# A third PSUM bank for the exponentials' scores, two shared banks for projections and output path

## The chip, the cores and the metric

The kernel runs on one core of one Trainium2 chip. The metric is the device time of one execution in microseconds (us). A core has a matrix engine (TensorE, PE in the rows; PEld is its weight load), a vector engine (DVE), a scalar engine (ACT), GpSimd (POOL), a queue engine for transfers (SP), and an accumulation memory, PSUM, of eight banks of 128 partitions x 512 float32 values. Only PE's results go there; ACT and DVE read them out. PE may overwrite a bank only once the last reader of what stood there is done, and it waits for that on a semaphore. PE executes its instructions in the order written.

## The reference

Two cross-attention layers after each other, batch of 4, 256 queries and 512 keys of width 256. The first has 16 heads of width 16 and an MLP of width 1024; the second one head of width 256 and a residual scaled by alpha.

```python
x = layer_norm(hidden_states, ln1_w, ln1_b)
q, k, v = x @ q_w + q_b, ctx @ k_w + k_b, ctx @ v_w + v_b      # 16 heads of 16
attn = softmax(where(mask, q k^T * scale, min))
hidden = (attn @ v) @ cproj_w + cproj_b + residual
y = gelu(layer_norm(hidden, ln2_w, ln2_b) @ fc_w + fc_b, approximate=True) @ proj_w + proj_b
x = hidden + y
# second layer, w_q, w_k, w_v, w_o of 256 x 256
probs = softmax((x @ w_q.T) @ (ctx @ w_k.T).T / sqrt(256))
out = x + alpha * ((probs @ (ctx @ w_v.T)) @ w_o.T)
```

## The kernel before

The four batches run one after the other through a pipeline that is written out by hand. The attention of one batch takes 32 slots, 8 for each of 4 groups of 4 heads (`slots`, `attend`). In nearly every slot PE makes one score tile of 128x512 whose maximum is wanted (`max_tile`, L562, tile `s1`; in slots 0 and 1 of a group two of them, in slots 6 and 7 none) and one score tile for the exponentials (`exp_tile`, L579, two matmuls, tile `s2`). DVE reduces the first kind to row maxima (`take_max`, L1331), ACT exponentiates the second (`exp`, L1009). In slot 5 of a group DVE splits the maxima of the next group into three bf16 parts (`split_max`, L1341 to L1347), in slot 6 PE transposes them (`max_rows`, L569) and ACT copies them into the operand of the next group's exponentials (`rows`, L1000). Twice a group PE multiplies probabilities by values (`pv`, L589).

Into these slots are threaded, by tables that name the slot of each step:

- the projections of the next batch (`pre`, `PRE_AT`): the transposed context in two halves CT0 and CT1 (L538), the transposed normalised input ZT (L533), then Q, K0, K1, V0, V1 (helper line L504). CT0 is at slot 7, CT1 at 8, ZT at 9, Q at 11, K0 at 14, K1 at 22, V0 at 36, V1 at 38. ACT copies a transposed tile and DVE subtracts the copy from it (L1301); K0 and K1 are read by DVE alone (L1310); V0 and V1 by ACT (L982);
- the output path of the batch before (`post`, `POST_AT`): OT0 and OT1, the transposed attention output in two halves, at slot 7 (L625), divided by the softmax sums on DVE (L1366, L1368); NT, CP, ZT; the MLP's four chunks F0 to F3; its second product in four parts PJ0 (slot 20), PJ1, PJ2 (slot 23), PJ3 (slot 25), which add up in one bank; the second layer's transposed context in halves, here called post-CT0 at slot 22 and post-CT1 at slot 24 (L618); then HT, G, S0, S1, PT0, PT1, PC and DL. The matmuls of these steps stand at the helper lines L517 and L521. `LATE_AT` spreads the same steps out for the third batch.

PE's order within a slot is: maximum tiles, `pre`, `post`, the exponentials' tile, `pv`, `max_rows`. The other engines follow the same slots, but read out most `pre` and `post` tiles on DVE one slot later; in a slot DVE takes `pre` ahead of `post`. The slots from 7 of one batch to 6 of the next are one iteration. Iteration 0 has projections and the preparation of weights (`prepare`), but no output path. Iterations 1 and 2 have both. In iteration 3 there is no further batch to project: the last batch's own output path (`tail`) runs beside the third batch's.

PSUM before: `s1` has 2 banks, `s2` 2, `om` (the attention output and the transposed maxima) 1, `pre_ps` 1, `post_ps` 2. The table `POST_BANK` gives each step of the output path one of its two banks.

Of the kernel before, what the change touches and what calls it, by code (L numbers as in the profile page):

```python
# [103 lines left out]
POST_BANK = (0, 1, 0, 1, 0, 1, 0, 1, 0, 1, 0, 0, 0, 1, 0, 1, 0, 1, 0, 1)  # L104
# [22 lines left out]
def build(nc, x, ctx, mask, ln1_w, ln1_b, q_w, q_b, k_w, k_b, v_w, v_b, cproj_w, cproj_b, ln2_w, ln2_b,  # L127
          fc_w, fc_b, proj_w, proj_b, l1_q, l1_k, l1_v, l1_o, alpha, out):
    with ExitStack() as stack:
# [176 lines left out]
        def bank_of(n):  # L306
            return POST_BANK[n]

# [7 lines left out]

        def pre_bank(b, n):

            if b == 0:
                return (pre_ps[:], post_ps[:, 0, :], post_ps[:, 1, :])[pre_place(b, n) % 3]  # L320
            return pre_ps[:]

        def post_use(b, n):

            bank = bank_of(n)
            return bank, POST_BANK.count(bank) * b + POST_BANK[:n].count(bank) + 1

# [56 lines left out]

        def steps_at(b):
            return LATE_AT if b == B - 2 else POST_AT

        def pre_at(b):
            return EARLY_AT if isinstance(b, int) and b == 1 else PRE_AT
# [109 lines left out]
        def _(pe):  # L499
# [55 lines left out]
            def max_tile(b, g, s):  # L555
# [5 lines left out]
                await_(pe, s1_free, n - 1)  # L561
                pe.matmul(s1[:, s % 2, :], q_stack[0:ROW_MAX, hd, chunk(t)], k_stack[0:ROW_MAX, hd, :],  # L562
# [9 lines left out]
            def exp_tile(b, g, s):  # L572
# [3 lines left out]
                await_(pe, s2_free, n - 1)  # L576
                for i in range(2):
                    k = 2 * (s % 2) + i
                    mm = pe.matmul(s2[:, s % 2, i * LQ:(i + 1) * LQ], k_stack[:, hd, chunk(k)], q_stack[:, hd, :],  # L579
                                   start=True, stop=True)  # L580
# [13 lines left out]
            def post(b, step):  # L594
                def open_(n):

                    bank, count = post_use(b, n)
                    await_(pe, post_free[bank], count)
                    return post_ps[:, bank, :]
# [10 lines left out]
                def fill(mm, n):  # L610
                    mm.then_inc(post_full[bank_of(n)], 1)
# [44 lines left out]
                elif step[:2] == "PJ":  # L656
                    i = int(step[2])
                    pe.wait_ge(y_hi, 4 * b + i + 1)
                    o = open_(W_PJ) if i == 0 else post_ps[:, bank_of(W_PJ), :]
# [1166 lines left out]
```

## Time and profile before

| | |
|---|---|
| median of three runs | 322.81 us |
| lowest, highest of the three | 320.57, 324.02 us |
| the profiled execution's own time | 322.9 us |
| its profiled span | 321.1 us |
| PE busy | 272.4 us, 85% of the span |
| DVE busy | 219.6 us, 68% |
| ACT busy | 188.6 us, 59% |
| mean granted clock of TensorE | 0.946 of full speed |

The profiled execution lies 0.1 us from the median. Between span and time lie 1.8 us. A time row of the trace gives a start and a duration in us from the span's start; a bracket behind it gives how long the engine had been idle and who ended that.

### The profile page before, as it was taken

The page shows a single profiled execution, that of the slowest core. Times are in us where ns is not written, and L with a number is a line of the kernel's source. Part 1 is how long each engine was busy: PE and PEld are TensorE (multiplying, and loading weights), DVE is VectorE, ACT ScalarE, POOL GpSimd, SP SyncE. Part 2 cuts the span into 40 slices and gives each one's busy share as a digit, 9 for nine tenths or more (in the row PEclk, how much of TensorE's full clock was granted, in tenths as well). Part 3 has the DMA queues.
Part 4 walks back from the last instruction along what each step waited for, and adds up shares of the span by engine and source line. Part 5 has one row for each costly group of instructions (what it writes and reads, how often), then busy time and mean ns, then how long its engine had stood idle before and what let it go on. Part 6 is the DMA issues. An engine that isn't in the chain of part 4 may idle for free.

```text
span 321.1 us, 5439 instructions
## 1 busy us (share of the span) xinstructions
PE 272.4 (85%) x2065; PEld 195.5 (61%) x2065; DVE 219.6 (68%) x433; ACT 188.6 (59%) x351; POOL 87.7 (27%) x85
## 2 busy tenths in 40 slices
PE   2936759999797979998979899989899988868995
PEld 2722435583274758764956757647767766657884
DVE  6756865758679678866488598674868744645844
ACT  2541635748765695967365877673637785325522
POOL 3311001503001387530022576700012271123300
PEclk9995878996799999999999999999999999969999
DMA  6299990292172029002630182018110000000000
GB/s 192 98 126 174 132 357 15 51 130 77 49 100 100 0 56 167 37 0 69 82 133 0 28 120 39 0 38 113 62 72 2 0 2 2 1 0 0 2 33 33
DMA packets 21805, 21.59 MB, mean 67 GB/s; under 512 B 2962, under 2 KB 18916, under 8 KB 21780
## 3 DMA queue, kind: packets, MB, share of 16 engines
q1 hardware_dynamic: 19488, 17.25, 29.3%
q10 hardware_dynamic: 2292, 4.01, 3.6%
q8 instruction: 16, 0.26, 0.4%
q14 instruction: 9, 0.07, 0.1%
HBM read 10.50 MB, written 1.05 MB: 36 GB/s over the span
## 4 chain that ended last, share of the span: by engine, by line
PE 44%; DVE 21%; ACT 15%; SPq 7%; issue 5%; POOL 4%; DMA 3%; ACTq 1%; DVEq 0%
PE post_ps L517 8%; PE om L589 7%; PE pre_ps L504 6%; DVE neg_max L1331 5%; PE s L562 4%; PE s L579 4%; PE post_ps L521 4%; ACT q_stack L1000 3%; ACT probs L1009 3%; SPq L431 2%; SPq L441 2%; PE s L517 2%; DMA cx<-in_ctx_dram 2%; DVE ft L1414 1%; DVE cT_l L1301 1%
## 5 line engine op out<-in xcount | busy, mean ns | idle before, releaser
L1331 DVE TENSOR_REDUCE neg_max<-s 128x1 f32<-128x512 f32 x128 | 83.2, 683 | 19.6 <-PE s L562 18.8
L1009 ACT ACTIVATE probs<-s 128x512 f32<-128x512 f32 x128 | 75.8, 599 | 23.9 <-PE s L579 23.4
L562 PE MATMUL s<-k_stack,q_stack 97*128 97x512 bf16 x128 | 49.7, 418 | 13.9 <-DMA q_stack<-qp 7.3
L579 PE MATMUL s<-q_stack,k_stack 109*128 109x256 bf16 x256 | 51.2, 283 | 2.7 <-ACT q_stack L1000 2.2
L562 PEld LDWEIGHTS s<-k_stack,q_stack 97*128 97x128 bf16 x128 | 12.6, 99 | 38.7 <-DVE neg_max L1331 20.2
L589 PE MATMUL om<-probs,vals 128*17 128x256 f32 x512 | 36.0, 404 | 0.0
L579 PEld LDWEIGHTS s<-q_stack,k_stack 109*128 109x128 bf16 x256 | 21.1, 101 | 16.3 <-ACT q_stack L1000 4.3
L1663 POOL TENSOR_TENSOR ln<-ln,minus_half 128x2 f32<-128x2 f32 x8 | 5.6, 704 | 82.8 <-DVE ln L1279 82.8
L1000 ACT ACTIVATE q_stack<-om 13x1024 bf16<-13x1024 bf16 x16 | 16.3, 1017 | 9.7 <-PE om L569 9.3
L589 PEld LDWEIGHTS om<-probs,vals 128*17 128x17 f32 x512 | 12.2, 100 | 14.5 <-issue 7.8
L1357 DVE TENSOR_TENSOR y_l<-post_ps,y_h 128x512 fp32r<-128x512 f32 x12 | 8.3, 689 | 16.2 <-ACT y_h L1023 16.2
L1023 ACT ACTIVATE y_h<-post_ps 128x512 fp32r<-128x512 f32 x12 | 7.0, 596 | 17.0 <-PE post_ps L521 13.7
L1414 DVE SCALAR_TENSOR_TENSOR ft<-ft,fx 128x512 f32<-128x512 f32 x9 | 12.0, 1333 | 7.2 <-POOL ft L1718 7.2
L1723 POOL TENSOR_TENSOR y_l<-fx,y_h 128x512 fp32r<-128x512 f32 x9 | 11.6, 1283 | 14.8 <-ACT y_h L1062 14.8
L1683 POOL TENSOR_TENSOR kf<-kf,kp 128x512 f32<-128x512 f32 x7 | 8.1, 1161 | 23.5 <-ACT kp L992 23.5
L1718 POOL TENSOR_TENSOR ft<-fx 128x512 f32<-128x512 f32 x9 | 9.4, 1043 | 15.6 <-ACT fx L1036 15.6
L517 PE MATMUL post_ps<-aT_h,wf_h 128*128 128x256 f32 x48 | 13.6, 316 | 0.0
L517 PE MATMUL post_ps<-wp_h,y_h 128*128 128x256 f32 x48 | 13.5, 313 | 0.1
L1705 POOL TENSOR_TENSOR h<-h,cb 128x512 f32<-128x512 f32 x3 | 3.8, 1277 | 32.7 <-DMA h<-in_x_dram 32.7
L517 PE MATMUL post_ps<-wp_l,y_h 128*128 128x256 f32 x48 | 11.8, 280 | 0.0
L517 PE MATMUL post_ps<-aT_h,wf_l 128*128 128x256 f32 x48 | 11.8, 280 | 0.0
L1687 POOL TENSOR_TENSOR kp<-kf,kp 128x512 bf16<-128x512 f32 x7 | 9.2, 1321 | 3.8 <-ACT kp L996 3.8
(327 smaller groups left out, 704.5 us busy)
## 6 DMA issues: line engine op xcount, KB each, us to landing
k_stack<-kp SPq DMA_DIRECT2D x48, 128.0 KB
q_stack<-qp SPq DMA_DIRECT2D x48, 64.0 KB
cx<-in_ctx_dram SPq DMA_DIRECT2D x4, 512.0 KB, 5.8
pcx<-in_ctx_dram ACTq DMA_DIRECT2D x3, 512.0 KB, 3.6
xz<-in_x_dram SPq DMA_DIRECT2D x5, 256.0 KB, 5.5
raw_late<-in_L_xattn_fc_w_dram SPq DMA_DIRECT2D x1, 1024.0 KB, 8.0
raw_late<-in_L_xattn_proj_w_dram SPq DMA_DIRECT2D x1, 1024.0 KB, 10.1
h<-in_x_dram ACTq DMA_DIRECT2D x3, 256.0 KB, 2.7
```

The source lines that it names most:

```text
L504: mm = pe.matmul(o, wi(w[a], k), vi(v[c], k), start=start and k == 0 and i == 0, stop=stop and k == n - 1 and i == 2)
L517: pe.matmul(o, wi(w[a], k), vi(v[c], k), start=start and i == k == a == c == 0, stop=False)
L521: mm = pe.matmul(o, wi(w[late[0]], k), vi(v[late[1]], k), start=False, stop=stop and i == len(terms) - 1 and k == n - 1)
L562: pe.matmul(s1[:, s % 2, :], q_stack[0:ROW_MAX, hd, chunk(t)], k_stack[0:ROW_MAX, hd, :], start=True, stop=True).then_inc(s1_full, 1)
L579: mm = pe.matmul(s2[:, s % 2, i * LQ:(i + 1) * LQ], k_stack[:, hd, chunk(k)], q_stack[:, hd, :], start=True, stop=True)
L589: mm = pe.matmul(om[32 * j:32 * j + VW, 0:LQ], vals[:, k, g * GH + j, :], probs[:, g % 2, j, k, :], start=k == 0, stop=k == TK - 1)
L1000: act.activation(q_stack[ROW_MASK:ROWS, g * GH:(g + 1) * GH, :], om_rows[ROW_MASK:ROWS, :].unsqueeze(1).to_broadcast([ROWS - ROW_MASK, GH, ...
L1009: act.activation(probs[:, g % 2, s // 2, k:k + 2, :], s2[:, s % 2, :].rearrange("p (k n) -> p k n", k=2), ACT.Exp).then_inc(s2_free, 1)
L1331: dve.tensor_reduce(neg_max[:, g % 2, s % 2, s // 2:s // 2 + 1], s1[:, s % 2, :], AX.X, ALU.max, negate=True).then_inc(s1_free, 1)
L1414: dve.scalar_tensor_tensor(f, f, 1.0 / GELU_CUBIC, fx[i % 3], ALU.add, ALU.mult).then_inc(cube, 1)
L1718: pool.tensor_tensor(ft[i % 3], fx[i % 3], fx[i % 3], ALU.mult).then_inc(square, 1)
L1723: pool.tensor_tensor(lo, fx[i % 3], hi.bitcast(F32), ALU.subtract).then_inc(y_split, 1)
```

## The change

All eight banks were in use and still are. `s2` gets a third bank. `pre_ps` and `post_ps` go, and a tile `work_ps` of two banks takes their place. A function `work_uses` lists every use of these two banks in PE's order (projections of the next batch, output path, three steps of the weight preparation) and deals them out in turn; while PJ0 to PJ3 add up in one bank, every other use goes to the other. `await_bank` makes each use wait until the use before it on its bank has been read out. The exponentials' tiles go round three banks in batches 0 to 2 and round two in batch 3, where the third serves the last output path. The first batch's projections use the third `s2` bank for every third tile and `work_ps` for the rest.

```diff
-POST_BANK = (0, 1, 0, 1, 0, 1, 0, 1, 0, 1, 0, 0, 0, 1, 0, 1, 0, 1, 0, 1)
...
-        s2 = ps("s2", [P, 2, 512])
+        s2 = ps("s2", [P, 3, 512])
         om = ps("om", [P, 512])
-        pre_ps = ps("pre_ps", [P, 512])
-        post_ps = ps("post_ps", [P, 2, 512])
-        tail_banks = [pre_ps[:], s1[:, 0, :], s1[:, 1, :], s2[:, 0, :], s2[:, 1, :], om[:]]
+        work_ps = ps("work_ps", [P, 2, 512])
+        spare_ps = s2[:, 2, :]
+        tail_banks = [spare_ps, s1[:, 0, :], s1[:, 1, :], s2[:, 0, :], s2[:, 1, :], om[:]]
...
+                    for use in new:
+                        bank = 1 - held if held is not None else 1 - bank
+                        uses.append(use + (bank,))
+                        if use[0] == "post" and use[2] == W_PJ:
+                            held = bank
+                    if step == "PJ3":
+                        held = None
...
+        def await_bank(eng, kind, b, n):
+
+            bank = work_bank(kind, b, n)
+            on = [u for u in WORK if u[3] == bank]
+            at = [u[:3] for u in on].index((kind, b, n))
+            if at == 0:
+                return
+            kind, b, n, _ = on[at - 1]
+            if kind == "pre":
+                eng.wait_ge(pre_free, PRE_USES if b == 0 else pre_use(b, n))
+            elif kind == "post":
+                eng.wait_ge(post_free[bank], post_use(b, n)[1] + 1)
...
+        def s2_bank(b, s):
+
+            return s % 2 if b == B - 1 else (NS * b + s) % 3
...
             def pre(b, n):
 
                 at = pre_place(b, n)
+                if b > 0:
+                    await_bank(pe, "pre", b, n)
                 await_(pe, pre_free, PRE_USES * b + n if b > 0 else max(at - 2, DC if n == U_K else U_ZT + 1) if n > U_ZT else at - 2)
...
-                await_(pe, s2_free, n - 1)
+                await_(pe, s2_free, s2_before(b, SLOTS * g + s))
...
-                    bank, count = post_use(b, n)
-                    await_(pe, post_free[bank], count)
-                    return post_ps[:, bank, :]
+                    await_bank(pe, "post", b, n)
+                    return work_ps[:, work_bank("post", b, n), :]
```

No instruction changes its place on any engine, and none is added but waits. Dealt out in turn, the uses of iteration 1 (and of 2, with the same banks) are, as bank 1: CT0, OT1, NT, CP, ZT of the output path, K0, F2, PJ, HT, S0, PT0, V0, DL; as bank 0: OT0, CT1, ZT of the projections, Q, F0, F1, F3, K1, post-CT0, post-CT1, G, S1, PT1, PC, V1. A projection keeps its old wait for the projection before it and gets the bank's wait beside it.

PE's rows at slots 7 and 8 of iteration 1, before (L538 is CT0, then CT1; L625 is OT0, then OT1; the semaphores in brackets are what the row waits for):

```order
L538 MATMUL pre_ps<-ident,cx 128x128 x3
L625 MATMUL post_ps<-ident,oT 128x128 [waits post_free0,o_done]
L625 MATMUL post_ps<-ident,oT 128x128 x3
L625 MATMUL post_ps<-ident,oT 128x128 [waits post_free1]
L625 MATMUL post_ps<-ident,oT 128x128 x3
L579 MATMUL s<-q_stack,k_stack 128x256 [waits s2_free]
L579 MATMUL s<-q_stack,k_stack 128x256
L562 MATMUL s<-k_stack,q_stack 128x512 [waits s1_free,stacked1]
L562 MATMUL s<-k_stack,q_stack 128x512 [waits s1_free]
L538 MATMUL pre_ps<-ident,cx 128x128 [waits cx_in,pre_free]
```

The same place in the change (L607 for L538, L696 for L625):

```order
L607 MATMUL work_ps<-ident,cx 128x128 x3
L696 MATMUL work_ps<-ident,oT 128x128 [waits pre_free,o_done]
L696 MATMUL work_ps<-ident,oT 128x128 x3
L696 MATMUL work_ps<-ident,oT 128x128 [waits pre_free]
L696 MATMUL work_ps<-ident,oT 128x128 x3
L651 MATMUL s<-q_stack,k_stack 128x256 [waits s2_free]
L651 MATMUL s<-q_stack,k_stack 128x256
L631 MATMUL s<-k_stack,q_stack 128x512 [waits s1_free,stacked1]
L631 MATMUL s<-k_stack,q_stack 128x512 [waits s1_free]
L607 MATMUL work_ps<-ident,cx 128x128 [waits cx_in,pre_free,post_free0]
```

OT1 waited for the output path's own bank and now waits for the projections' CT0 to be read out; CT1 waits for OT0 as well.

PE's rows at slots 22 and 23 of iteration 1, before (L504 is the end of K1, L618 post-CT0, L569 the transposed maxima, L517 the start of PJ2):

```order
L504 MATMUL pre_ps<-cT_h,wk_l 128x512
L618 MATMUL post_ps<-ident,pcx 128x128 [waits post_free0,pcx_in]
L618 MATMUL post_ps<-ident,pcx 128x128 x3
L579 MATMUL s<-q_stack,k_stack 128x256 [waits s2_free]
L579 MATMUL s<-q_stack,k_stack 128x256
L569 MATMUL om<-ident_b,max_cols 109x128 [waits o_done,max_split]
L569 MATMUL om<-ident_b,max_cols 109x128
L517 MATMUL post_ps<-wp_h,y_h 128x256 [waits y_hi]
```

The same place in the change:

```order
L571 MATMUL work_ps<-cT_h,wk_l 128x512
L689 MATMUL work_ps<-ident,pcx 128x128 [waits pre_free,pcx_in]
L689 MATMUL work_ps<-ident,pcx 128x128 x3
L651 MATMUL s<-q_stack,k_stack 128x256 [waits s2_free]
L651 MATMUL s<-q_stack,k_stack 128x256
L638 MATMUL om<-ident_b,max_cols 109x128 [waits o_done,max_split]
L638 MATMUL om<-ident_b,max_cols 109x128
L584 MATMUL work_ps<-wp_h,y_h 128x256 [waits y_hi]
```

Nothing moved; post-CT0 waited for the output path's bank 0 and now waits for K1, the use right ahead of it, to be read out by DVE, since PJ holds the other bank.

## Rows read from the trace of the kernel before

**Rows 1.** The page: the span, and each engine's busy us.

```profile
span 321.1 us, 5439 instructions
PE 272.4 (85%) x2065; PEld 195.5 (61%) x2065; DVE 219.6 (68%) x433; ACT 188.6 (59%) x351; POOL 87.7 (27%) x85
```

**Rows 2.** Windows, iterations 1 and 2: busy us of PE, PEld, DVE, ACT, POOL; clock; DMA.

```profile
94.00:161.00 67.00, 60.77 (x499) 44.52 (x497) 49.01 (x97) 44.35 (x84) 24.14 (x20) 1.00 0.33 62
161.00:228.00 67.00, 60.73 (x498) 44.47 (x497) 49.38 (x98) 44.37 (x84) 25.42 (x21) 1.00 0.31 57
```

**Rows 3.** Waits of PE: waiting line, released by; us in total, times, longest.

```profile
PE s L579 <- ACT probs L1009: 0.4, 2, 0.2
```

**Rows 4.** Line L579, PE and PEld together: idle us before it, times, until.

```profile
  ACT probs L1009: 2.6, 8
```

**Rows 5.** Timeline of PE, iteration 0: start, us, what, idle before and releaser.

```profile
54.80 0.38 PE L579 MATMUL s<-q_stack,k_stack 109*128 109x256 bf16 x2
...
55.02 0.38 PE L562 MATMUL s<-k_stack,q_stack 97*128 97x512 bf16 x1
...
55.56 0.11 PEld L579 LDWEIGHTS s<-q_stack,k_stack 109*128 109x128 bf16 x2 [0.55 <-ACT probs L1009]
```

**Rows 6.** Timeline, iteration 1, slots 7 and 8.

```profile
95.51 1.04 PE L625 MATMUL post_ps<-ident,oT 128*128 128x128 f32 x8
...
97.15 0.69 DVE L1301 TENSOR_TENSOR cT_l<-pre_ps,cT_h 128x512 fp32r<-128x512 f32 x1 [0.50 <-ACT cT_h L966]
...
97.89 0.66 PE L538 MATMUL pre_ps<-ident,cx 128*128 128x128 f32 x4 [0.69 <-DVE cT_l L1301]
...
98.38 0.25 DVE L1366 RECIPROCAL rden<-post_ps 128x16 f32<-128x16 f32 x1
98.59 0.60 ACT L966 ACTIVATE cT_h<-pre_ps 128x512 fp32r<-128x512 f32 x1 [0.98 <-PE pre_ps L538]
...
99.00 1.28 DVE L1331 TENSOR_REDUCE neg_max<-s 128x1 f32<-128x512 f32 x2
```

**Rows 7.** Timeline, iteration 1, slots 22 and 23.

```profile
128.75 0.40 PE L504 MATMUL pre_ps<-cT_h,wk_l 128*128 128x512 f32 x1
...
128.99 0.60 PE L618 MATMUL post_ps<-ident,pcx 128*128 128x128 f32 x4
...
129.42 0.39 PE L579 MATMUL s<-q_stack,k_stack 109*128 109x256 bf16 x2
...
130.14 0.32 PE L569 MATMUL om<-ident_b,max_cols 128*109 128x128 bf16 x2 [0.34 <-DVE max_cols L1347]
...
130.60 0.74 DVE L1310 SCALAR_TENSOR_TENSOR kf<-pre_ps,bk,mask_f 128x512 f32<-128x512 f32 x1
```

**Rows 8.** Chain that ended last, iteration 1: start, us, what.

```profile
130.14 0.32 PE om L569 x2
130.46 1.00 PE post_ps L517 x8
```

**Rows 9.** Timeline, iteration 2, slot 23.

```profile
197.55 0.74 DVE L1310 SCALAR_TENSOR_TENSOR kf<-pre_ps,bk,mask_f 128x512 f32<-128x512 f32 x1
```

**Rows 10.** Timeline, iteration 1: K0's reader on DVE, start of F2.

```profile
113.43 0.74 DVE L1310 SCALAR_TENSOR_TENSOR kf<-pre_ps,bk,mask_f 128x512 f32<-128x512 f32 x1
...
114.54 0.47 PE L517 MATMUL post_ps<-aT_h,wf_h 128*128 128x256 f32 x1
```

**Rows 11.** Windows, as rows 2; the third number from the end is the granted clock.

```profile
70.00:94.00 24.00, 21.63 (x149) 10.58 (x149) 17.47 (x32) 17.32 (x28) 2.56 (x2) 0.79 0.45 85
...
264.00:267.00 3.00, 1.30 (x19) 0.81 (x11) 2.71 (x4) 1.34 (x4) 1.08 (x1) 1.00 0.00 0
...
283.00:290.00 7.00, 6.05 (x28) 5.71 (x29) 1.35 (x4) 1.44 (x3) 1.04 (x1) 0.51 0.00 0
```

**Rows 12.** Timeline of PE: two long idle times in iteration 3.

```profile
266.22 0.41 PE L756 MATMUL s<-ident,mask_f 128*128 128x128 f32 x2 [1.70 <-DVE mask_f L1578]
...
283.17 1.09 PE L777 MATMUL s<-ident,mask_f 128*128 128x128 f32 x4 [2.32 <-DVE mask_f L1285]
```

More of the change, by code:

```diff
@@ L315, in pre_use, with work_uses @@
             return PRE_USES * b + pre_place(b, n) + 1
+        def work_uses():
+            uses, bank, held = [], 1, None
+            for n in FIRST_ORDER:
+                if pre_place(0, n) % 3:
+                    uses.append(("pre", 0, n, pre_place(0, n) % 3 - 1))
+            for b in range(B):
+                for at in range(START, LAST_SLOT if b == B - 1 else START + NS):
+                    new = []
+                    if b < B - 1 and at in pre_at(b + 1):
+                        new.append(("pre", b + 1, pre_at(b + 1)[at]))
+                    if b < B - 1 and at in V_AT:
+                        new.append(("pre", b + 1, U_V + V_AT[at]))
+                    step = steps_at(b - 1).get(at) if b > 0 else None
+                    new += [("post", b - 1, n) for n in STEP_USES.get(step, ())]
+                    if b == 0 and PREP_AT.get(at) in PREP_USES:
+                        new.append(("prep", 0, PREP_AT[at]))
+                    for use in new:
[5 more added lines that the diff above has]
+                        held = None
+            return uses
@@ L317, in pre_bank, with work_bank @@
+        WORK = work_uses()
+        def work_bank(kind, b, n):
+            return [u[3] for u in WORK if u[:3] == (kind, b, n)][0]
         def pre_bank(b, n):
-            if b == 0:
-                return (pre_ps[:], post_ps[:, 0, :], post_ps[:, 1, :])[pre_place(b, n) % 3]
-            return pre_ps[:]
+            if b == 0 and pre_place(b, n) % 3 == 0:
+                return spare_ps
+            return work_ps[:, work_bank("pre", b, n), :]
         def post_use(b, n):
-            bank = bank_of(n)
@@ L326, in post_use @@
-            return bank, POST_BANK.count(bank) * b + POST_BANK[:n].count(bank) + 1
+            bank = work_bank("post", b, n)
+            return bank, [u[1:3] for u in WORK if u[0] == "post" and u[3] == bank].index((b, n)) + 1
+        def await_bank(eng, kind, b, n):
[9 more added lines that the diff above has]
+                eng.wait_ge(post_free[bank], post_use(b, n)[1] + 1)
+            elif n == "WO":
+                eng.wait_ge(w_lo, 4)
+            else:
+                eng.wait_ge(prep_done, 1 if n == "WT" else 2)
@@ new lines, in s1_bank, with s1_before, s2_before @@
+        def s1_bank(b, s):
+            return s % 2
+        def s1_before(b, s):
+            n = NS * b + s
+            return max([i for i in range(max(0, n - 3), n) if s1_bank(i // NS, i % NS) == s1_bank(b, s)], default=-1) + 1
+        def s2_bank(b, s):
+            return s % 2 if b == B - 1 else (NS * b + s) % 3
+        def s2_before(b, s):
+            n = NS * b + s
+            return max([i for i in range(max(0, n - 3), n) if s2_bank(i // NS, i % NS) == s2_bank(b, s)], default=-1) + 1
@@ L1052, in exp1 @@
                 act.wait_ge(cx_split, b + 1)
-                act.activation(probs1(b)[:, t, :], post_ps[:, bank, :], ACT.Exp, bias=stat1[:, 0, t:t + 1],
+                act.activation(probs1(b)[:, t, :], work_ps[:, bank, :], ACT.Exp, bias=stat1[:, 0, t:t + 1],
                                accum_out=stat1[:, 1, t:t + 1]).then_inc(post_free[bank], 1)
```

72 lines of the change are left out of this document (39 added, 33 removed).

## The prediction

> **What bounds the kernel now.** The page's busy times come first [rows 1]: PE works 272.4 of 321.1 us, DVE 219.6, ACT 188.6. PE is the busiest, and its share is an average. The windows by stage show that iterations 1 and 2 take 67 us each, with PE busy for 60.77 and 60.73 us at full granted clock [rows 2]. So in the two iterations where the output path and the next projections share the change's two banks, PE has only some 6 us to spare, and a wait put on PE there will mostly be added to the time. The second view is PE's waits, read for the one wait that a third score bank takes away: an exponentials' tile that waits for ACT to read an older one. PE's matmuls sat idle for it twice, 0.4 us in all [rows 3]; with the weight loads, which carry the semaphore and often wait while PE still streams the matmul ahead, it is 2.6 us in 8 places [rows 4]. The third view is the timeline at every use of the shared banks. For each I compared the start of the use with the end of the instruction that reads out the use now ahead of it on its bank. Where the start is later, the new wait is covered. It is clearly earlier at two places in an iteration, OT1 at slot 7 [rows 6] and post-CT0 at slot 22 [rows 7]. The chain of work that ended last passes through the second [rows 8].
>
> **The third score bank: 0.3 us gained.** What it can give is bounded by nothing from below (if PE's pause only moves to the next wait) and by the 2.6 us of rows 4 from above. I looked for places where the chain goes from an exponential to the next exponentials' tile. There is one: in iteration 0 the tile of slot 13 starts at 55.56 with its weight load idle for 0.55 us [rows 5]. The matmul ahead of it starts at 55.02, and a step from a pair of exponentials' matmuls to the next instruction is 55.02 - 54.80 = 0.22 us, so with a free bank it starts at 55.24, 0.3 us earlier. In iterations 1 and 2 PE reaches its exponentials' tiles later than ACT frees the banks. There the third bank gives nothing at first hand. I take 0.3 us.
>
> A rule of the Trainium skill speaks for more: Perfetto Trace Analysis, section Optimization Strategy, says that the same gap repeating on the engine that should be saturated can mean there is not enough PSUM for the next tile. Were the 2.6 us of rows 4 such gaps, the change would give 2.6 us by that rule; by the rows on PE's matmuls it is 0.4 us, so these are not the gaps that matter here.
>
> **OT1 waits for the projections' CT0: 0.2 us lost, twice.** The eight transposes of OT0 and OT1 run together from 95.51 to 96.55. CT0 is read out when DVE's subtraction ends, 97.15 + 0.69 = 97.84, and PE starts what waited for that 0.05 us later, at 97.89 [rows 6]. OT1 therefore starts at 97.89 instead of about 95.95. Queued behind it on PE are the exponentials' tile, the two maximum tiles of slot 8, and CT1, which itself waits until 97.89 today. PE's new order from 97.89: OT1 takes 0.43 (as post-CT0's four transposes from 128.99 to 129.42 [rows 7]), the exponentials' tile 0.22, the two maximum tiles 0.22 each, so CT1 starts at 98.98, 1.1 us later than now. But the chain runs over DVE here. Its reciprocal for OT1 starts at 98.38 [rows 6]; OT1 is now full at 97.89 + 0.60 = 98.49, so with a few hundredths for the signal it starts at about 98.57: 0.2 us later. Behind it the two reductions of 1.28 us now start at 99.20 and end at 100.48. ACT copies CT1 at 98.59 + 1.1 = 99.69 to 100.29, before DVE is free to use it. So CT1's 1.1 us are hidden by the two reductions, with 0.2 us to spare; without that cover it would be 1.1 us. I take 0.2, with 1.1 as upper end and 0 as lower (if DVE catches up in a later pause).
>
> **Post-CT0 waits for K1: 1.9 us lost, twice.** K1's last matmul ends at 128.75 + 0.40 = 129.15, and PE goes on with post-CT0 at 128.99. K1 is read out by DVE one slot later, after the row maxima of the next group have been split and after a step of the MLP's gelu: from 130.60 to 131.34 [rows 7]. PJ holds the other bank, so post-CT0 may start at 131.34 + 0.05 = 131.39, 2.4 us later. Queued behind it on PE are the exponentials' tile of slot 22 and the transposes of the maxima, which start at 130.14, as soon as DVE has split them. Now they start at 131.39 + 0.43 + 0.22 = 132.04: 1.9 us later. What DVE does until 131.34 needs nothing that stands behind the wait, so the 131.34 stays. The transposes are on the chain, and what follows on the chain is PE itself, part PJ2 [rows 8]; on ACT the copy of post-CT0, the exponential and the copy of the maxima queue up and come 2.5 us late, but ACT is idle for a third of this iteration (44.35 of 67 [rows 2]) and need not carry that on. The stall of 1.9 us thus runs through to the end. Iteration 2 shows the same pattern 66.95 us later: DVE's reading of K1 starts at 197.55 [rows 9] against 130.60. So twice 1.9 = 3.8 us. The lower end is 1.0 each (third rival), the upper 2.4, the whole delay of post-CT0.
>
> **The other uses: nothing.** The other new neighbours on a bank are covered in the trace. The tightest is F2, which starts at 114.54 where K0 is read out at 113.43 + 0.74 = 114.17 [rows 10]: 0.4 us of cover. All of them move together with the delays above, so the cover stays; if F2's were gone it would be some tenths, since ACT is the later one there. In iteration 3 there are no projections to share with, and iteration 0 has no output path. 17 waits are added in front of PE's groups, 10 of them in iterations 1 and 2. A group with two waits starts no later in these rows than one with one, so they cost nothing at best; at worst the 0.2 us of a step each, 2 us.
>
> **Sum.** 322.9 (the profiled execution's own time) - 0.3 + 2 x 0.2 + 2 x 1.9 = 326.8 us. The median of the three runs is 322.8, so the same sum from there gives 326.7. I predict 326.8. This case's own range is 325.2 to 328.6: less 1.6 for stalls that are partly absorbed, more 1.8 for OT1's missing cover (2 x 0.9).
>
> **Rivals.**
>
> *The clock falls.* The new pause of PE ahead of post-CT0 is 131.39 - 129.15 = 2.2 us long. In iteration 3 an idle time of 1.70 us left the granted clock at 1.00, and one of 2.32 us [rows 12] stands ahead of a stretch of 7 us at 0.51 [rows 11], which is the lower level, 1.2 GHz. The new pause lies between, nearer the longer. Against it: ahead of the 2.32 us PE had been idle in several more places, while ahead of post-CT0 it works without a gap. A stretch of 7 us at half the clock where PE is busy nine tenths of the time costs 7 x 0.49 = 3.4 us: 330.2 us if it happens once, 333.6 if in both iterations. Chance 16 in 100. The page TensorE: Matmul & The Clock Gate of the Trainium skill, section A second HAM failure mode: psum-queue depth-cycling, says that a kernel whose PE paused briefly between groups while it cycled through PSUM banks went back and forth between the two clock levels; here the trace of before, with pauses such as 0.69 and 0.34 us [rows 6, 7], shows the granted clock at 1.00 in both iterations [rows 2].
>
> *The stall is partly absorbed.* Iterations 1 and 2 have some 6 us each in which PE is idle [rows 2]. If later pauses of PE belong to chains that the delay doesn't touch, they swallow part of it, and about 1 us of each 1.9 is left: 322.9 - 0.3 + 0.4 + 2.0 = 325.0 us, within 1%. Against it speaks that the chain is on PE itself right behind the stall. Chance 20 in 100.
>
> *Faster: PE runs ahead in iteration 0.* The stretch from 70 to 94 us has a mean granted clock of 0.79 [rows 11]; the missing 0.21 of 24 us are 5.0 us. If the third bank closes the pauses of the weight loads (2.6 us) and with them keeps the clock up, the kernel gains 7.6 us against 4.2 lost: 319.5 us. It decides from a gain of 7.4 us on (3.2 for the 1% and 4.2 for the stalls), so nearly all of both would have to come. The chain crosses this stretch with ACT's exponentials and weight copies back to back, and a bank makes ACT no faster. Chance 6 in 100.
>
> **How the numbers follow.** My forecast has 56 in 100, the rivals 16, 20 and 6, and 2 are left for what I don't see. A measurement of this kernel tells about 1% from no change: below 319.6 is faster, above 326.0 slower. Of the 56, about 44 lie above 326.0 and 12 below; with the clock's 16 and 1 of the rest, slower is 0.61, within 1% is 0.12 + 0.20 + 0.01 = 0.33, faster 0.06. The range for 8 in 10 goes from 323.9 (the absorbed case, with a further microsecond) to 330.4 (the clock falling once).
>
> **What the changed kernel's profile would show.** If I am right: PE's row for the transposes of post-CT0 has an idle time of about 2 us released by DVE's read of K1, once in each of iterations 1 and 2; OT1's four transposes stand apart from OT0's with about 1.7 us of idle time, and CT1's no longer wait; the reductions behind OT1 are 0.2 us late; iterations 1 and 2 are each about 2 us longer than 67 and iteration 0 is as long as before within 0.5 us; PE no longer waits for ACT ahead of exponentials' tiles. The prediction is wrong if the granted clock falls in iterations 1 or 2, if iteration 0 becomes shorter by more than 1 us, or if the delay at slot 22 is there and the iteration has its old length.

## The result, and the profile after

The changed kernel took 330.72 us (median of 4 executions, 328.67 to 334.46) beside 321.88 us for the kernel before: a ratio of 1.0223, with a 95% interval of 1.0169 to 1.0277. (The ratio leaves out executions in a slower state, here the profiled one; the two medians alone would give 1.027.)

Measured again later, with more executions, it was 333.12 us, ratio 1.034 [1.0287, 1.0392]. The two intervals of the same kernel don't touch, so a difference of about 0.01 between two kernels that were not measured together says nothing. A part of it can be the clock: the mean granted clock of the three executions in the first ratio is 0.940, that of the six in the second 0.927. Ratios are compared below. e1, e2, e3 and e5 were measured together on one chip, e4, e6, e7 and e8 on a second, e9 to e12 on a third.

The profiled execution took 334.46 us, 3.7 above its median, so a sum made on its trace must be read against that; the trace of the second measurement (335.12 us, the same granted clock of 0.917) looks alike.

The page after, as [rows 1]. PE's busy time rises by 7 us with the same 2065 matmuls; DVE, ACT and POOL do what they did.

```profile
span 332.7 us, 5456 instructions
PE 279.5 (84%) x2065; PEld 203.2 (61%) x2065; DVE 220.4 (66%) x433; ACT 188.3 (57%) x351; POOL 87.6 (26%) x85
PEclk9975858969797999999989998999999997968999
```

The same PEclk line of the page of the kernel before (40 slices, granted clock in tenths):

```profile
PEclk9995878996799999999999999999999999969999
```

The mean granted clock of the profiled execution is 0.917, where the kernel before had 0.946. The windows of iterations 1 and 2, to be held against [rows 2], and of three short stretches, against [rows 11] (columns: stretch, its length, busy us of PE, PEld, DVE, ACT, POOL, granted clock, DMA share, GB/s):

```profile
96.00:166.50 70.50, 61.96 (x497) 45.60 (x495) 49.27 (x96) 44.33 (x84) 24.15 (x20) 0.98 0.29 58
166.50:237.00 70.50, 62.06 (x487) 45.57 (x486) 48.41 (x93) 43.84 (x83) 25.46 (x21) 0.95 0.29 53
...
99.80:103.20 3.40, 3.40 (x16) 2.74 (x16) 2.35 (x5) 1.05 (x2) 0.00 (x0) 0.51 0.33 82
171.50:174.90 3.40, 3.32 (x15) 2.26 (x14) 2.46 (x5) 1.88 (x4) 0.44 (x1) 0.50 0.59 158
205.70:209.10 3.40, 3.40 (x19) 3.28 (x17) 0.69 (x1) 2.73 (x4) 0.09 (x1) 0.51 0.02 5
```

These windows are cut by hand. By the ends of the same exponentials' tiles in both traces, iterations 1 and 2 are 3.8 and 4.9 us longer than before, not 2. The three short stretches stand at 1.2 GHz, the lower level, right behind three of the four new pauses. PE is busy through all of them (3.32 to 3.40 of 3.40 us), and the trace of the second measurement has the same three, at 100.3, 171.9 and 206.1. The waits of PE (line, releaser: us in total, times, longest):

```profile
PE work_ps L689 <- DVE kf L1383: 4.7, 2, 2.3
PE work_ps L696 <- DVE cT_l L1374: 3.5, 2, 1.8
```

These are post-CT0, which waits for K1's reader, and OT1, which waits for CT0's reader. The row of [rows 3], exponentials' tiles that wait for ACT, has no answer after: that wait is gone. Timeline of iteration 1, slots 7 and 8, as [rows 6] (start, us, engine, line, what; in brackets the idle time before it and the releaser):

```profile
97.25 0.60 PE L696 MATMUL work_ps<-ident,oT 128*128 128x128 f32 x4
...
98.87 0.69 DVE L1374 TENSOR_TENSOR cT_l<-work_ps,cT_h 128x512 fp32r<-128x512 f32 x1 [0.56 <-ACT cT_h L1039]
99.62 0.95 PE L696 MATMUL work_ps<-ident,oT 128*128 128x128 f32 x4 [1.76 <-DVE cT_l L1374]
100.37 0.63 PE L651 MATMUL s<-q_stack,k_stack 109*128 109x256 bf16 x2
100.61 0.26 DVE L1439 RECIPROCAL rden<-work_ps 128x16 f32<-128x16 f32 x1 [0.43 <-PE work_ps L696]
101.47 1.29 DVE L1404 TENSOR_REDUCE neg_max<-s 128x1 f32<-128x512 f32 x2
101.65 1.06 PE L607 MATMUL work_ps<-ident,cx 128*128 128x128 f32 x4
```

OT0's four transposes took 0.60 us, and OT1's, the same work behind 1.76 us of idle time, 0.95. The exponentials' tile behind them took 0.63, where 0.39 stands in [rows 7], and CT1's four transposes 1.06 instead of 0.66 [rows 6]. These rows lie in the stretch at 0.51. Slots 22 and 23 of iteration 1, as [rows 7]:

```profile
134.10 0.75 DVE L1383 SCALAR_TENSOR_TENSOR kf<-work_ps,bk,mask_f 128x512 f32<-128x512 f32 x1
134.99 0.63 PE L689 MATMUL work_ps<-ident,pcx 128*128 128x128 f32 x4 [2.33 <-DVE kf L1383]
135.68 0.28 PE L638 MATMUL om<-ident_b,max_cols 128*109 128x128 bf16 x2
```

The chain that ended last, as [rows 8] (start, us, what), now enters the place over DVE's reading of K1:

```profile
134.18 0.67 DVE kf L1383
134.85 0.14 issue
134.99 0.63 PE work_ps L689 x4
135.62 0.22 PE s L651 x2
135.84 0.11 PE om L638 x2
135.95 1.00 PE work_ps L584 x8
```

Comparing the end of every exponentials' tile between the two traces shows where the 11.6 us (332.7 - 321.1) of the profiled execution arise: iteration 0 1.7 (the tiles fall behind where a low-clock stretch starts at 69.1 instead of 71.4), OT1 1.8 in iteration 1 and 1.4 in iteration 2, post-CT0 2.0 in iteration 1 and 3.6 in iteration 2, the last iteration about 1.2 (a low-clock stretch from 277.3 that the kernel before doesn't have).

### The profile page after: what moved, and what is told of

Same layout as the page of the kernel before. It is cut to its first block, busy times and chain, and to the rows that moved or that the text cites. A ratio compares the mean times of both kernels' runs of the same rounds, so it can differ in the third digit from the quotient of the medians.

```text
span 332.7 us, 5456 instructions
## 1 busy us (share of the span) xinstructions
PE 279.5 (84%) x2065; PEld 203.2 (61%) x2065; DVE 220.4 (66%) x433; ACT 188.3 (57%) x351; POOL 87.6 (26%) x85
## 4 chain that ended last, share of the span: by engine, by line
PE 47%; DVE 20%; ACT 14%; SPq 6%; issue 5%; POOL 4%; DMA 3%; ACTq 1%; DVEq 0%
PE work_ps L584 9%; PE om L661 7%; DVE neg_max L1404 5%; PE s L631 5%; PE s L651 4%; PE work_ps L588 4%; PE work_ps L571 4%; ACT probs L1082 3%; SPq L498 2%; SPq L508 2%; PE s L584 2%; ACT q_stack L1073 2%; DMA cx<-in_ctx_dram 2%; DVE ft L1487 1%; PE work_ps L925 1%
## 5 line engine op out<-in xcount | busy, mean ns | idle before, releaser
L651 PE MATMUL s<-q_stack,k_stack 109*128 109x256 bf16 x256 | 52.2, 290 | 2.2 <-ACT q_stack L1073 2.1
L661 PE MATMUL om<-probs,vals 128*17 128x256 f32 x512 | 35.2, 396 | 0.0
L651 PEld LDWEIGHTS s<-q_stack,k_stack 109*128 109x128 bf16 x256 | 22.1, 104 | 15.5 <-ACT q_stack L1073 4.2
L1430 DVE TENSOR_TENSOR y_l<-work_ps,y_h 128x512 fp32r<-128x512 f32 x12 | 8.3, 689 | 16.2 <-ACT y_h L1096 16.2
L1796 POOL TENSOR_TENSOR y_l<-fx,y_h 128x512 fp32r<-128x512 f32 x9 | 11.6, 1285 | 20.0 <-ACT y_h L1135 20.0
L1096 ACT ACTIVATE y_h<-work_ps 128x512 fp32r<-128x512 f32 x12 | 7.0, 596 | 17.0 <-PE work_ps L588 13.7
L584 PE MATMUL work_ps<-wp_h,y_h 128*128 128x256 f32 x48 | 14.7, 335 | 0.0
L584 PE MATMUL work_ps<-aT_h,wf_h 128*128 128x256 f32 x48 | 13.6, 316 | 0.0
L584 PE MATMUL work_ps<-wp_l,y_h 128*128 128x256 f32 x48 | 13.1, 300 | 0.0
L584 PE MATMUL work_ps<-aT_h,wf_l 128*128 128x256 f32 x48 | 11.8, 280 | 0.0
L1430 DVE TENSOR_TENSOR pT_l<-work_ps,pT_h 128x512 fp32r<-128x512 f32 x6 | 4.2, 692 | 11.1 <-ACT pT_h L1100 11.0
```

The costliest lines, as they stand in the source:

```text
L584: pe.matmul(o, wi(w[a], k), vi(v[c], k), start=start and i == k == a == c == 0, stop=False)
L651: mm = pe.matmul(s2[:, s2_bank(b, SLOTS * g + s), i * LQ:(i + 1) * LQ], k_stack[:, hd, chunk(k)], q_stack[:, hd, :], start=True, stop=True)
L661: mm = pe.matmul(om[32 * j:32 * j + VW, 0:LQ], vals[:, k, g * GH + j, :], probs[:, g % 2, j, k, :], start=k == 0, stop=k == TK - 1)
L1430: dve.tensor_tensor(dst, work_ps[:, work_bank("post", b, n), :].rearrange("p (c n) -> p c n", c=dst.shape[1]), hi.bitcast(F32), ALU.subtra ...
L1796: pool.tensor_tensor(lo, fx[i % 3], hi.bitcast(F32), ALU.subtract).then_inc(y_split, 1)
```

## The experiments

Two theories stood against each other at the start. **A, waits alone:** the added time is the sum of the two pauses, and the banks' order sets it. **B, waits and clock:** a pause is paid once as a wait, and often again as a stretch at half clock behind it. (In the recorded expectations "Theory A" is the name of the view stated there, mostly that the two waits, with or without their clock, carry the loss. A and B below are the two of this paragraph.) A third question ran beside them: does the third score bank give anything? In e1 to e5 and e11 the exponentials' tiles use two banks again, and the eighth bank, called spare, is free for other use.

### Only the third score bank undone

`e1_two_score_banks`: the change with two score banks, the eighth bank idle. `e6_change_again` is the second measurement of the change itself, on another chip than e1.

```diff
-            return s % 2 if b == B - 1 else (NS * b + s) % 3
+            return s % 2
```

> The change with the third score bank left unused by the exponentials (two banks as in the kernel before), the two shared banks kept: what is left is the sharing alone. Theory A (the loss is two waits on the shared banks, OT1 and post-CT0, and the low-clock stretches that they bring; the third bank gives nothing): slower than before by the same 7 us as the change, within 1 us. Rival (the third bank gives the 2.6 us of weight-load waits and hides part of the sharing's cost): about 2.5 us slower than the change, 9.5 us over before.

> The change itself once more, beside the other three on one chip. By its first measurement 7.2 us over before (ratio 1.022). The kernel with two score banks gave a ratio of 1.033. Theory A (the third score bank gives nothing): here it comes out at 1.033 as well, within 0.005. Rival (the third bank gives about 3 us, more than the 0.3 us of the prediction): 1.022 again.

Measured: 332.35 us, ratio 1.0326 [1.0276, 1.0375], against 1.034 [1.0287, 1.0392] of the change. **The third bank gives nothing that can be measured**; the first measurement of the change, 1.0223, lies lower than both, so a gain is only possible as far as that difference between the two measurements leaves it open. The loss, 10.5 us here where 7 were expected, is there without the third bank, so it belongs to the two shared banks. The wait of PE for K1's reader in e1, and the windows behind its two pauses (columns as above):

```profile
PE work_ps L689 <- DVE kf L1383: 4.7, 2, 2.3
```

```profile
132.00:135.40 3.40, 2.67 (x23) 2.54 (x24) 1.27 (x2) 1.99 (x3) 0.00 (x0) 1.00 0.00 0
...
203.00:206.40 3.40, 3.40 (x19) 3.24 (x17) 0.69 (x1) 2.74 (x4) 0.37 (x1) 0.50 0.02 5
```

The same pause ahead of post-CT0 (2.34 us in each iteration) is followed by full clock in iteration 1 and by 3.4 us at half clock in iteration 2. The delay that arises there, by the ends of the exponentials' tiles, is 1.98 us in the first case and 3.55 in the second. One trace thus holds both prices: 2.0 for the wait, 1.6 more where a fall follows. The 1.6 is one pair of cases; e2, with a fall in both iterations, has 3.55 and 3.51. OT1's wait adds 0.27 us at once in both iterations.

### Each disputed use in a bank of its own

On top of e1, the spare bank takes the projections' CT0 (e2), K1 (e3) or both (e4) of batches 2 and 3, and nothing waits for or behind them.

```diff
+        def spared(kind, b, n):
+            return kind == "pre" and b >= 2 and n in (U_CT,)         # e3: (U_K + 1,)   e4: (U_CT, U_K + 1)
...
+                    new = [u for u in new if not spared(*u)]
...
-            if b == 0 and pre_place(b, n) % 3 == 0:
+            if spared("pre", b, n) or b == 0 and pre_place(b, n) % 3 == 0:
...
-                if b > 0:
+                if b > 0 and not spared("pre", b, n):
```

> As the run with two score banks, but the projections' CT0 of batches 2 and 3 goes to the idle eighth bank, so that OT1 no longer waits for it to be read out. Theory A with the prediction's price (OT1's wait costs 0.2 us an iteration beside the clock): 0.4 us faster than with two score banks, if the clock stays as it is. Theory A with the clock (the 1.8 us pause ahead of OT1 is followed by a stretch at the lower clock in both iterations, 3.5 us at half speed): 3 us faster, PEclk 1.00 after 94 us up to the second wait. Rival (sharing costs are spread over all uses): no change over 0.5 us.

Measured: 331.32 us, 1.0269 [1.0217, 1.032]; 0.006 less than e1, 1.8 us, with intervals that overlap, so that it does not decide between the expected 0.4 and 3 us. Here the clock fell in iteration 1 too, and post-CT0's wait cost 3.55 us there instead of e1's 1.98. Window of e2:

```profile
131.50:134.90 3.40, 3.29 (x16) 3.20 (x17) 0.69 (x1) 2.11 (x4) 0.00 (x0) 0.50 0.02 5
```

> As the run with two score banks, but K1 of batches 2 and 3 goes to the idle eighth bank, so that post-CT0 no longer waits for DVE to read it. Theory A: the 2.3 us pause ahead of post-CT0 goes in both iterations, 2 x 1.9 = 3.8 us faster than with two score banks, up to 1.6 us more where a low-clock stretch followed. Rival (the delay is absorbed later): under 2 us faster.

Measured: 324.63 us, 1.0067 [1.0029, 1.0106]. **Taking K1 alone out of the shared banks gives back 1.0326 - 1.0067 = 0.026, 8.4 us.** That is more than the 3.8 to 5.4 us expected. Its windows of iterations 1 and 2 stand at full clock, and by the tiles' ends they are 0.4 and 0.8 us longer than before:

```profile
94.00:162.00 68.00, 61.36 (x504) 45.15 (x503) 49.76 (x100) 44.42 (x86) 24.18 (x20) 1.00 0.33 62
162.00:229.00 67.00, 59.86 (x492) 43.78 (x491) 48.88 (x96) 44.30 (x84) 25.42 (x21) 1.00 0.31 56
```

> Two score banks, and both CT0 and K1 of batches 2 and 3 in the eighth bank, so that neither OT1 nor post-CT0 waits. All other uses still share two banks. Theory A (two waits carry all of the loss): the time of before, within 1 us. Rival (the other shared uses and the added waits of PE cost too): 2 us or more over before. The run that freed K1 alone was 2.2 us over before; if OT1's wait is the rest, this one is 1.5 to 2 us faster than that.

Measured: 323.9 us, 1.004 [1.001, 1.0071]. All the other shared uses and added waits together are worth 1.3 us, 0.3 to 2.3 by the interval. 8.4 us is twice what two waits of 2 us can explain. But it does not yet say that the rest is the clock, because an own bank also removes whatever else hangs on the wait.

### The waits kept, the pauses filled

`e5_fill_pauses`: e1 with every wait in its place, and ahead of each of the four waiting groups matmuls that nobody reads, into the spare bank. Their results are not used, so nothing that is computed changes. The first loop stands ahead of post-CT0, the second ahead of OT1.

```diff
+                    if c == 0 and b < B - 2:
+                        for _ in range(18):
+                            pe.matmul(spare_ps[:, 0:LQ], wq[0][:, 0, 0:P], wq[0][:, 0, :], start=True, stop=True)
...
+                        if t == 1 and b < B - 2:
+                            for _ in range(14):
+                                pe.matmul(spare_ps[:, 0:LQ], wq[0][:, 0, 0:P], wq[0][:, 0, :], start=True, stop=True)
```

> As the run with two score banks, with matmuls that nobody reads into the idle eighth bank right ahead of the two waits (14 of 128x256 ahead of OT1, 18 ahead of post-CT0, about 1.65 and 2.1 us at the higher clock), so that PE waits equally long but busy. This separates the wait from the clock. Theory A with the clock: no low-clock stretch behind 94 us before the last iteration, and 2 to 3 us faster than with two score banks, about 4.2 us over before, as the prediction's sum had it. Theory A without the clock (the low stretches come anyway, wherever they fall): the same time as with two score banks, or up to 1 us slower.

Measured: 326.0 us, 1.0128 [1.0086, 1.017]. Timeline of iteration 1:

```profile
128.37 2.32 PE L689 MATMUL s<-wq_h 128*128 128x256 f32 x18
130.79 0.66 PE L692 MATMUL work_ps<-ident,pcx 128*128 128x128 f32 x4
131.50 0.28 PE L638 MATMUL om<-ident_b,max_cols 128*109 128x128 bf16 x2
```

and the windows of iterations 1 and 2:

```profile
92.00:162.00 70.00, 65.30 (x537) 49.31 (x536) 49.84 (x101) 44.96 (x87) 24.17 (x20) 1.00 0.36 65
162.00:232.00 70.00, 65.27 (x538) 49.24 (x537) 50.19 (x99) 44.42 (x85) 25.42 (x21) 1.00 0.29 54
```

Post-CT0 is as late as in e1 (the delays are 1.94 and 1.93 us), and the clock stays at 1.00. **With the waits unchanged and the pauses filled, 1.0326 becomes 1.0128, 6.4 us less.** This tells A from B: the waits alone don't make the 10.5 us (0.0326 x 322.7) of e1. What the filled kernel costs, 0.0128 x 322.7 = 4.1 us, is about what the sum of the prediction had for the waits.

The split into 6.4 us of clock and 4.1 us of waits is that of whole executions, and not all of the 6.4 arises behind the four pauses. The mean granted clock is 0.927 over the six executions of e1, 0.953 over those of e5, and 0.946 over the 17 of the kernel before on that chip. With 2 x (1 - clock) x span, an estimate of the time at half clock, these are 48, 30 and 35 us. Four stretches of 3.4 us are 13.6 of the 18 us between e1 and e5, so part lies elsewhere, and e5 even has less of it than the kernel before. In the two traces iterations 1 and 2 together are 6.7 us longer than before in e1, with one fall, and 4.6 in e5; a further 1.9 us lie in iteration 0, where both run the same program. So it is shown that the lower clock costs e1 several us beside its waits; how much of that belongs to the four pauses stays open.

`e11_k1_own_fill_ot1` is e3 with the 14 matmuls ahead of OT1.

> Two score banks, K1 in the eighth bank, and 14 matmuls that nobody reads ahead of OT1's wait, so that OT1's pause stays and its idle time goes. With K1's own bank alone the ratio was 1.0067, with both in own banks 1.004. If OT1's wait costs through the clock: 1.004 here too, or less. If it costs through its delay alone: 1.007.

Measured: 323.75 us, 1.0028 [0.9994, 1.0062], beside e3's 1.0067 [1.0029, 1.0106]: about 1.3 us less, as B has it, but the intervals overlap and the chips differ, so this shows nothing by itself.

### Moving the output path instead

`e7_move_ct0` leaves the banks as in the change and puts post-CT0 two slots later, behind K1's reader; `e8_move_both` also puts the projections' CT0 a slot later, behind OT.

```diff
-           21: "PJ1", 22: "CT0", 23: "PJ2", 24: "CT1", 25: "PJ3", 26: "CX", 27: "HT", 28: "G", 30: "S0",
+           21: "PJ1", 23: "PJ2", 24: "CT0", 25: "PJ3", 26: "CT1", 27: "HT", 28: "G", 29: "CX", 30: "S0",
...
-PRE_AT = {7: U_CT, 8: U_CT + 1, 9: U_ZT, 11: U_Q, 14: U_K, 22: U_K + 1}
+PRE_AT = {8: U_CT, 9: U_CT + 1, 10: U_ZT, 12: U_Q, 14: U_K, 22: U_K + 1}
```

(The second pair of lines is e8's alone. Its expectation says that batches 1 and 3 follow this table; in fact batch 1 has the early table, and batches 2 and 3 follow this one, in iterations 1 and 2.)

> The change with three score banks, and the steps of the second layer's context moved in the table: post-CT0 from slot 22 to 24, post-CT1 from 24 to 26, CX from 26 to 29. DVE has read K1 by slot 23, so post-CT0 finds its bank free without a bank of its own. Theory A: the same gain as from K1's own bank, 5 to 8 us faster than the change, the idle time ahead of post-CT0 gone. Rival (the delay moves on: CX at 29 makes the second layer's exponentials at slot 31 wait for POOL's subtraction of 2.4 us): under 3 us faster, with a wait at the transposes PT0.

Measured: 333.57 us, 1.031 [1.0247, 1.0373], where 5 to 8 us less than the change were expected. A miss. The pause ahead of post-CT0 was gone, and a new one stood ahead of the transposes of the maxima. Timeline of e7, iteration 1:

```profile
140.80 2.34 POOL L1806 TENSOR_TENSOR pc_l<-pcx,pc_h 128x1024 fp32r<-128x1024 f32 x1 [6.96 <-ACT pc_h L1147]
140.86 2.31 DVE L1416 TENSOR_TENSOR max_rest<-neg_max,max_cols 128x8 f32<-128x8 f32 x1
143.65 0.32 PE L638 MATMUL om<-ident_b,max_cols 128*109 128x128 bf16 x2 [2.42 <-DVE max_cols L1420]
```

DVE's subtraction of 8 elements, 0.17 to 0.18 us elsewhere, took 2.31: it ended with POOL's large subtraction, and the transposes of the maxima waited 2.42 us for it. In iteration 2 they waited 3.43 us: there the same subtraction took 2.31 us again, and the cast behind it (L1418, also 128x8) took 1.20 instead of 0.18, beside a POOL instruction of 1.26 us on `xz`. The move gave one pause of PE for another.

> As the run with moved post-CT0, and the projections' CT0, CT1, ZT and Q of batches 1 and 3 one slot later (8, 9, 10, 12), so that OT0 and OT1 take the two banks first and CT0 follows when OT0 has been read. Batch 2 keeps its early slots by its own table, so OT1's wait goes in one of the two iterations. Theory A: 0.3 to 1 us faster than with post-CT0 moved alone. Rival: the shift puts Q's reading and F0 onto each other and costs 1 us or more.

Measured: 336.95 us, 1.0453 [1.0408, 1.0497]. The worst of all: it keeps e7's pauses, and in place of OT1's comes one of 1.62 us ahead of the transposes of z in each iteration, and in iteration 1 one of 2.02 ahead of a maxima tile.

`e9_swap` exchanges post-CT0 with the next PJ parts; `e12_before_swap` makes the same exchange in the kernel before.

```diff
-           21: "PJ1", 22: "CT0", 23: "PJ2", 24: "CT1", 25: "PJ3", 26: "CX", 27: "HT", 28: "G", 30: "S0",
+           21: "PJ1", 22: "PJ2", 23: "CT0", 24: "CX", 25: "PJ3", 26: "CT1", 27: "HT", 28: "G", 30: "S0",
```

> The change, with PJ2 in slot 22 and post-CT0 in slot 23 instead of the other way round; CX goes from 26 to 24 and post-CT1 from 24 to 26, so that the order of the other steps stays. PJ2's 1.5 us of matmuls then stand where PE waited for K1 to be read. Theory A: the pause of 2.3 us ahead of post-CT0 goes and nothing takes its place; what is left is OT1's wait: ratio to before 1.005 to 1.012, as with K1's own bank (1.007). Rival (DVE's row maxima or the transposes come later behind PJ2 and the loss stays): over 1.02.

> The kernel before with the same exchange of PJ2 and post-CT0 (and CX, post-CT1 at 24 and 26). PE then has PJ2 to do while DVE splits the maxima (idle 0.34 us at 129.81 in the trace of before). Expected: the same time within 1 us; at best 2 x 0.3 us faster, at worst 2 x 0.9 us slower, since the transposes of the maxima come behind PJ2's 1.5 us.

Measured: e9 333.81 us, 1.0348 [1.0296, 1.0399]; e12 333.2 us, 1.0315 [1.0263, 1.0366]. Both expectations were missed. The order of e9 costs the kernel before, which has three banks for these uses, 10 us of its own. With that order, going to two banks costs 0.0033 more, within the intervals. So what two banks cost hangs on which use stands next to which, and most of this order's loss is not that of the change. It comes from another pause. Waits, timeline and chain of e12:

```profile
PE s L562 <- DVE neg_max L1331: 10.9, 18, 2.2
```

```profile
132.50 1.21 PE L562 MATMUL s<-k_stack,q_stack 97*128 97x512 bf16 x2 [2.20 <-DVE neg_max L1331]
```

```profile
130.52 0.61 ACT pT_h L1027
131.15 0.69 DVE pT_l L1357
131.84 0.60 DVE neg_max L1331
132.50 1.21 PE s L562 x2
```

DVE now reads post-CT0 before it reduces the maxima, and PE waits 2.2 us for the maxima's bank. The two matmuls behind that pause take 1.21 us, twice the 0.60 of full clock (0.38 and a step of 0.22, [rows 5]): the low clock again, in the kernel with the old banks. By the tiles' ends each of e12's iterations 1 and 2 is 4.8 us longer than before. Some 1.3 us of that arise at slot 27 and not in e9: `POST_BANK` gives post-CT1 and HT the same bank, the exchange brings post-CT1 to the slot right ahead of HT's, and HT's transposes wait 1.07 us for DVE to read post-CT1 (139.57). So e9 and e12 lose by pauses that are in part different ones, and 0.0033 is not the pure price of two banks in this order.

`e10_swap_three_s1` is e9 with the third bank given to the maxima's tiles; the exponentials have two, and the waits on the spare bank follow it.

```diff
-        s1 = ps("s1", [P, 2, 512])
-        s2 = ps("s2", [P, 3, 512])
+        s1 = ps("s1", [P, 3, 512])
+        s2 = ps("s2", [P, 2, 512])
...
         def s1_bank(b, s):
 
-            return s % 2
+            return s % 2 if b == B - 1 or b == 0 and s < SLOTS else (NS * b + s) % 3
```

> As the run with PJ2 and post-CT0 exchanged, but the third score bank serves the maximum tiles that DVE reduces, and the exponentials have two. The trace of before has PE idle for 6.4 us ahead of maximum tiles and 0.4 us ahead of exponentials' tiles. If a bank is worth what PE waits for: up to 6 us faster than the exchange alone, 3 us faster than before. If the chain is DVE's own work there, so that PE's running ahead changes nothing (what the exponentials' bank showed for ACT): the same as the exchange alone within 1 us.

Measured: 330.75 us, 1.0257 [1.0199, 1.0315], some 3 us (0.0091 x 322.9) under e9, with intervals that just overlap. PE's waits for the maxima in e9, and then in e10:

```profile
PE s L631 <- DVE neg_max L1404: 10.8, 19, 2.1
```

```profile
PE s L633 <- DVE neg_max L1406: 7.6, 13, 1.5
PE work_ps L691 <- DVE kf L1385: 2.1, 2, 1.0
```

The last row shows that PE in e10 reaches post-CT0 early enough to wait for K1's reader again, 1.0 us each time. None of the experiments' kernels is faster than the kernel before; e11 is level with it.

### How often the clock fell

Pauses of 1.76 or 1.77 us ahead of OT1 (14 in seven traces: the change twice, e1, e3, e7, e9, e10) were followed 7 times by a stretch of 3.4 us at 0.50 or 0.51. Pauses of 2.33 to 2.36 us ahead of post-CT0 (8 in the change twice, e1 and e2) were followed by one 5 times: once in 4 in iteration 1, 4 in 4 in iteration 2. The 12 other pauses above 1.5 us in iterations 1 and 2 (e7 to e10 and e12) were followed by one 6 times: not those of 2.42 and 3.43 us in e7, but those of 2.1 to 2.2 us in e9 and e12, the 3.44 us of e8's iteration 2, and the one of 1.53 us in e10. A stretch is counted where it begins up to 1.5 us behind the pause's end, or in e12 up to 0.3 us ahead of it. Behind the places that were filled in e5 there was none in 4. The pause of 1.70 us in the last iteration [rows 12] is 1.93 to 1.99 us long in all twelve traces with two shared banks, and a low stretch followed it in seven. What decides between the two outcomes at one length stays open.

## Where the prediction held and where it missed

The direction was right, and so were the two places and the price of the waits; the clock was not. 326.8 us was 3.9 too low against 330.72, and by the ratios the change cost 7.2 and 11.0 us (0.0223 and 0.034 x 322) where the sum had 3.9. The range of 323.9 to 330.4 holds the first ratio by a little (1.0223 x 322.9 = 330.1), though not the median itself, and it doesn't hold the second (333.9). That the first measurement fell inside is luck: the range was drawn for one fall at 3.4 us, and what came were several at less. By its own sign ("wrong if the granted clock falls in iterations 1 or 2") the forecast case did not come about. The step that failed is the rival *the clock falls*: as the prediction put it, "Chance 16 in 100", and only ahead of post-CT0.

- **The clock: mis-judged in chance and in place.** The argument against it was that PE "works without a gap" ahead of post-CT0. It did, and the clock fell in 5 of 8 cases. The anchor was one pause of 1.70 us without a fall. But the sum itself puts OT1's transposes from 95.95 to 97.89, a pause at least as long (1.76 us measured), and the prediction never weighed the clock there; it fell after 7 of 14. The price of one fall was set at 3.4 us, from a stretch of 7 us. The stretches are 3.4 us long and cost about 1.6 (e1, 3.55 against 1.98). So one fall is half as dear as said and came more often. With the waits held fixed and the pauses filled the kernel is 6.4 us faster (e5 against e1), part of it outside the four places.
- **Post-CT0's wait: right.** 1.9 forecast for each; 1.98 in e1 and 1.94 and 1.93 in e5 where the clock kept up. PE's pause was 2.33 us, forecast 2.2. The stall ran through to the end undiminished, so the rival *partly absorbed* fell.
- **OT1's wait: too small.** 0.2 forecast; 0.27 arose at once in e1 and e5 and 0.35 to 0.87 four to six tiles later; 1.4 and 1.8 in the change, where the clock fell. The reductions' cover for CT1 had 0.2 us to spare by the sum, which is less than a low clock adds to CT1's transposes (1.06 instead of 0.66).
- **The sum of the waits: right.** Forecast 2.1 us for each iteration; in e5's trace, without low clock there, iterations 1 and 2 are about 2.3 us longer each. That e5 comes to 1.0128 x 322.7 = 326.8, the forecast itself, is closer than the single terms warrant: e5 has two score banks, its last iteration keeps a low stretch, and its executions had less half clock than the kernel before.
- **The third score bank: nothing instead of 0.3.** The change against e1 shows no gain. PE's row of waits for the exponentials is gone as forecast, and it was not on the path. The rule on repeated gaps cited there (the Trainium skill, Perfetto Trace Analysis, section Optimization Strategy) does not fit this place, as the rows said; a third bank for the maxima, ahead of which PE really waited, gave some 3 us in e10, if the just overlapping intervals are taken at their middles.
- **Other uses and 17 waits: nothing, nearly right.** With K1 and CT0 out of the way 0.4% is left (e4), 1.3 us, inside the 0 to 2 us given.
- **Iteration 0 as before within 0.5 us: not in this trace.** It was 1.7 us late. This iteration has one to three low-clock stretches of its own in every kernel here, on other work in each: the kernel before has them at 44.1 to 50.9, 71.4 to 78.2 and 85.1 to 88.5 us, the change at 41.8 to 52.1, 69.1 to 75.9 and 86.2 to 89.6. The other traces lie from 3.1 us early (e7) to 2.1 us late (the change again) at its end. e1 and e5 are the same program in this iteration, and one is 0.9 us late, the other 1.0 early. So these traces don't make it a cost of the change; a part of it can't be excluded.
- **Faster because PE runs ahead in iteration 0:** did not come about; by the same comparison the change is late there and not early.
- **The range:** its lower end was set at 1.6 us under the sum, where the bounds given for the single terms (twice 0.9, and 0.2 for OT1 twice) add up to 2.2. Nothing depended on it.

The other page cited, TensorE: Matmul & The Clock Gate of the Trainium skill, section A second HAM failure mode: psum-queue depth-cycling, describes what came about: a PE that pauses between groups over PSUM banks and goes back and forth between the levels. The traces of the change agree, with three stretches at 0.50 or 0.51 behind four new pauses. The trace of before, with pauses of 0.34 and 0.69 us at full clock, said nothing of longer ones, though the prediction set it against that page.

## What to carry to other kernels

Where a busy PE must wait for a shared bank, price the wait twice: its length where the chain crosses it, and a chance of one half (18 of 34 pauses of 1.5 to 3.4 us here) of 1.6 us more for the clock. For the four pauses here that makes 3.4 us beside the 4.2 of the waits, 7.6 in all. That is near the change's first measurement (7.2) and short of its second (11.0) and of e1 (10.5), so it is a lower estimate. Compare every new pause with the trace's own pauses, those off the chain too, and treat the row nearest in length as one draw, not as a limit. Before taking a bank from a rotation, look for the use whose reader runs a slot later than its writer, here K1: giving that one alone its own bank gave back 8.4 of 10.5 us, where a third score bank gave nothing.

## What the hardware showed unexpectedly

- The granted clock fell to 0.50 for 3.4 us behind pauses as short as 1.76 us, and 1.53 in one case, in a PE busy for nine tenths of the iteration, and not behind every one. With 14 and 18 matmuls whose output nobody reads in the same pauses it stood at 1.00 in both iterations, and the kernel was 6.4 us faster than with the same waits idle.
- A DVE subtraction of 128 x 8 elements took 2.31 us instead of 0.17 while POOL subtracted 128 x 1024: POOL ran from 140.80 to 143.14, DVE from 140.86 to 143.17. The Trainium skill, page SBUF — State Buffer, section SBUF: two separate sides, says that a DVE operation with two inputs in SBUF and a POOL operation that reads SBUF share one port pair, held for a whole instruction. The rows of e7 agree with that: the later of the two was done only when the earlier one was. Moving CX by three slots was enough to bring them together. In iteration 2 a cast of 128 x 8 with a single input took 1.20 us instead of 0.18 beside another POOL instruction; why, no run here shows.
